# The last stage of a graph layer: routing and combining seven groups of nodes in three parts in place of two

## The chip, the cores and the metric

The kernel runs on one core of a Trainium2 chip. The metric is the time of one execution on the device in microseconds. Three executions of the kernel before took 3125.85, 3130.18 and 3136.21 us, a median of 3130.18 us.

## The reference

One layer of a graph transformer on 6250 nodes of 256 features, in float32. Cut to its frame and to the end of its feed-forward half, which is what the last stage computes:

```python
xn = _layernorm(x, axis=-1)
x = x + _L0_gnn_ref(xn, src, dst, ...) + _L0_mix_ref(xn[None], ...)[0]      # 100000 edges, linear attention
x = x + _L0_ffn_ref(_layernorm(x, axis=-1)[None], ...)[0]                   # 131072 edges + loops
...
# inside _L0_ffn_ref: h has 4 heads x 4 experts = 16 numbers per node
agg = segment_sum(msg, dst).reshape(M, 16) + b_gat                          # softmax-weighted over incoming edges
scores = _layernorm(agg, ln_gamma, ln_beta).reshape(M, HEADS, NUM_EXPERTS).mean(1)
topk_s, topk_i = lax.top_k(scores, 2)
w = softmax(topk_s)
out = 0
for ei in range(4):
    g = where(topk_i == ei, w, 0).sum(-1)
    hh = gelu(x @ W1[ei] + b1[ei], approximate=False)
    out = out + g[..., None] * (hh @ W2[ei] + b2[ei])
```

## The kernel before, in words

The nodes are 49 tiles of 128 (6250 padded to 6272). The long stages ahead, which gather rows for every edge and compute all four experts for every node, take the first 2981 us of the profile; they write two arrays to DRAM that the last stage reads: `state_ffn`, the running softmax state after every edge, and `y`, the four expert outputs of every node (4 x 256 numbers). `x1` holds the node features to which the result is added.

The last stage is the function `finish` (L2211). It splits the 49 tiles into 7 groups of G = 7 tiles. What each engine's program does there, in its own order:

- SP (L2260 to L2267) loads three small parameter rows, then `y` of group 0, then all of `x1` (`fin_x`, 6272 KB), then `y` of groups 1 and 2 (each 3584 KB). `fin_y` has three slots, so `y` of group b (b = 3 to 6) is loaded only once group b - 3 has been combined (semaphore `ready`).
- POOL (L2270 to L2275) issues 49 indirect gathers of the nodes' states, one per tile, in order of tiles. Each group has its own semaphore `got[q]`.
- DVE (L2325 to L2444) does for each group: `shift(q)` (L2336, waits for `got[q]`, three small operations), `merge(q)` (L2346, waits for ACT's exponentials, eight operations; it joins the gathered state with the node's own loop and divides). Within a part, `shift(q + 1)` comes before `merge(q)`. Once per part it does `route(part)` (L2364): a layer norm over the 16 numbers, the mean over heads, the ranks of the four experts, the two best and their weights. Each of its operations covers all tiles of the part at once, and behind nearly each comes a drain, since each reads what the last wrote. Then for each group of the part it does `combine(b)` (L2415): four tiles of the group by 16 scalar_tensor_tensor operations, and three tiles by adding what TensorE has mixed in PSUM.
- PE (L2278 to L2291) multiplies, for three tiles of each group, the four expert outputs by diagonal matrices of the gate weights. Each matmul of float32 operands is two instructions in the profile.
- ACT (L2293 to L2322) does the exponentials for the shifts (L2307), the square root and one exponential in each route (L2309, L2311; each ahead of them loads its table), the diagonal matrices (`spread_gates`, L2294, 12 activations for a group, for the first group of a part only after `routed`), and issues the store of each combined group (L2319).

`PARTS` (L2219) lists the groups of each part. All three programs that loop over parts (ACT, DVE and the helper `tiles`) take it from there. Before, part 0 has groups 0 to 2 and part 1 has groups 3 to 6. The order on DVE is thus: shift and merge of groups 0 to 2, route of 21 tiles, combine of groups 0 to 2, shift and merge of groups 3 to 6, route of 28 tiles, combine of groups 3 to 6. Nothing else sets the order; there is no planner.

Of the kernel before, what the change touches and what calls it, by code (L numbers as in the profile page):

```python
# [101 lines left out]
class Kernel:  # L102
# [2108 lines left out]
    def finish(self, own_h, own_m, out):  # L2211
# [4 lines left out]
        C, S, K = g.cols, g.state, g.per_head  # L2216
        G = FFN_BLOCK
        groups = NT // G
        PARTS = ((0, 3), (3, groups))  # L2219
        BY_PE = (G - 3, G - 2, G - 1)  # L2220
        with ExitStack() as here:
            x, yv = self.fin_x, self.fin_y
# [34 lines left out]
            def tiles(part):  # L2257
                return slice(PARTS[part][0] * G, PARTS[part][1] * G)

# [33 lines left out]
            def _(act):  # L2293
                def spread_gates(b):  # L2294
                    for n, u in enumerate(BY_PE):
# [5 lines left out]
                        ins.then_inc(spread, 1)  # L2301
                for part, (first_group, end) in enumerate(PARTS):
                    at = tiles(part)
# [21 lines left out]
            def _(dve):  # L2325
# [105 lines left out]
                dve.memset(eps[:, :], EPS)  # L2431
                for part, (first_group, end) in enumerate(PARTS):
                    for q in range(first_group, end):
# [96 lines left out]
```

How the kernel before makes its waits and increments, by code:

```python
            @block.vector  # L204
            def _(dve):
                dve.memset(self.edge_src["ffn"][:, :], 0)
                for g in (GNN, FFN):
                    dve.memset(self.start_rows[g.name][:, :, 0:1], 1.0)
                    dve.memset(self.start_rows[g.name][:, NT, 1:1 + H], 0.0)
                dve.wait_ge(counted, 1)
                dve.tensor_copy(lane[:, :], lane_i[:, :])
                dve.tensor_copy(tile_at[:, :], tile_i[:, :])
                dve.tensor_copy(node_at[:, :], node_i[:, :])
# [36 lines left out]
            def sp_samples(sp):  # L251
                table = self.sample_dram[g.name]
                sp.dma_start(here[:, :], table[:, :]).then_inc(samples_in, 16)
                sp.wait_ge(above_clear, 1)
                sp.dma_start(above[1:P, :], table[0:P - 1, :]).then_inc(samples_in, 16)
# [9 lines left out]
            def dve_rise(dve):  # L265
                dve.wait_ge(samples_in, 32)
                dve.tensor_tensor(rise[:, :], here[:, :], above[:, :], ALU.subtract)
                dve.memset(parts[:, 0, S:S + 1], 1.0)
                dve.memset(parts[:, 1, S:S + 1], 0.0)
# [12 lines left out]
            def pe_samples(pe, later, banks):  # L283
                pe.wait_ge(first_made, 1)
                pe.wait_ge(rise_ready, 1)
                for a, b, out in by_bank(banks):
                    for t in range(a, b):
# [4 lines left out]
            def dve_blocks(dve, banks, few):  # L293
                dve.wait_ge(samples_made, 1)
                for a, b, out in by_bank(banks):
```

## Time and profile before

| what | us |
|---|---|
| median of three executions | 3130.18 (3125.85 to 3136.21) |
| the profiled execution: its own time | 3130.82 |
| its span, first to last instruction | 3129.1 |
| last stage, from DVE's first operation in it to the end of the span | 2980.98 to 3129.1 |
| last operation of DVE ends | 3120.64 |

All positions are us from the span's start. A row of the chain or of the timeline has the start, the duration, the engine, the line and what the operation writes and reads; what stands in brackets is the idle time of the engine ahead of it and what ended that. An engine's name with a q (SPq, ACTq) is its issuing side: DMA issues stand there and aren't counted as busy.

### The profile page before, as it was taken

Reading aid. Unit: us, or ns where it says so; the run is one execution under the profiler, and the core shown is the slowest. Engines: PE = TensorE matmul, PEld = TensorE weight load, DVE = VectorE, ACT = ScalarE, POOL = GpSimd, SP = SyncE. Lnnn points to the kernel's source line nnn. Section 1 sums busy time; section 2 is a strip of 40 time slices with the busy share of each in tenths; the row PEclk is TensorE's granted clock in tenths of the full one; section 3 lists DMA queues with packets and bytes.
Section 4 is the critical chain, followed back from the end, with each engine's and each line's share of the span. In section 5 each row is a group of like instructions: output and inputs, shape, how many; then the busy total and the mean of one; then the engine's idle time right before and its main releaser. Section 6 shows DMA issues by size and latency. Waiting matters only on the chain. (4 is left out here: it accounts for less than half of the span.)

```text
span 3129.1 us, 19146 instructions
## 1 busy us (share of the span) xinstructions
PE 1313.0 (42%) x4490; PEld 883.1 (28%) x4490; DVE 1691.9 (54%) x2849; ACT 1207.3 (39%) x2380; POOL 2155.8 (69%) x2142
## 2 busy tenths in 40 slices
PE   2757611222222222221341566666666666661023
PEld 1523410111111111110330344444444444441012
DVE  7978899988888888884854111111111111111147
ACT  1522357766666676663430222222222222221012
POOL 0565657777777777776676777777777777777660
PEclk9878855555555555555555788888888888886557
DMA  4512646766666666665523122222222211122176
GB/s 130 189 54 74 194 135 227 235 209 209 217 212 216 220 211 210 211 218 189 165 61 100 30 42 42 42 42 42 42 42 42 42 37 37 36 42 47 17 255 247
DMA packets 223040, 392.05 MB, mean 125 GB/s; under 512 B 52803, under 2 KB 175346, under 8 KB 215504
## 3 DMA queue, kind: packets, MB, share of 16 engines
q1 hardware_dynamic: 132948, 258.07, 24.0%
q0 software_dynamic: 80880, 124.27, 16.9%
q10 hardware_dynamic: 9100, 8.50, 0.8%
q8 instruction: 36, 0.59, 0.1%
q14 instruction: 76, 0.62, 0.1%
HBM read 201.15 MB, written 189.55 MB: 125 GB/s over the span
## 5 line engine op out<-in xcount | busy, mean ns | idle before, releaser
L1217 POOL DMA_INDIRECT stage_got<-ffn_rows,setup_src_ffn x1024 | 985.0, 962 | 311.9 <-issue 311.9
L1217 POOL DMA_INDIRECT edges_got<-gnn_rows,edges_src_gnn x728 | 758.2, 1041 | 240.7 <-issue 221.5
L2099 PE MATMUL stage_ph<-ffn_xt_all,stage_w 128*128 128x448 f32 x896 | 408.1, 598 | 468.2 <-ACT stage_hid L2150 202.3
L1324 DVE TENSOR_TENSOR_SCAN stage_y<-stage_decays,stage_y 128x960 f32<-128x960 f32 (+2 forms) x256 | 521.1, 2090 | 5.1 <-issue 5.0
L1340 ACT ACTIVATE stage_rows<-stage_y 128x3640 f32<-128x3640 f32 (+1 forms) x88 | 399.9, 4544 | 0.0
L2099 PEld LDWEIGHTS stage_ph<-ffn_xt_all,stage_w 128*128 128x128 f32 x896 | 182.7, 208 | 615.2 <-ACT stage_start_parts L2150 203.8
L1233 DVE TENSOR_TENSOR stage_chunk_parts<-stage_got,edges_ffn_ed_edge 128x128 f32<-128x128 f32 x32 | 13.3, 416 | 592.3 <-DMA stage_got<-ffn_rows,setup_src_ffn 592.3
L1613 PE MATMUL stage_pm<-setup_ident,stage_mix_parts 128*128 128x128 f32 x98 | 33.4, 445 | 676.8 <-DVE stage_mix_parts L1686 604.2
L2176 DVE TENSOR_TENSOR search_found<-stage_po,stage_b 128x512 f32<-128x512 f32 x112 | 69.7, 625 | 420.9 <-PE stage_po L2110 416.1
L1282 ACT ACTIVATE stage_y<-stage_chunk_parts 128x56 f32<-128x56 f32 (+1 forms) x88 | 23.8, 271 | 670.4 <-DVE stage_chunk_parts L1254 669.9
L1300 DVE TENSOR_TENSOR stage_y<-edges_got,stage_y 128x896 f32<-128x896 f32 x168 | 262.9, 1671 | 0.3 <-ACT stage_y L1282 0.3
L1613 PEld LDWEIGHTS stage_pm<-setup_ident,stage_mix_parts 128*128 128x128 f32 x98 | 14.2, 204 | 706.4 <-DVE stage_mix_parts L1686 678.7
L1311 ACT ACTIVATE stage_y<-edges_got,stage_y 128x64 f32<-128x64 f32 x784 | 195.3, 388 | 0.0
L2110 PE MATMUL stage_po<-stage_w,stage_hid 128*128 128x256 f32 x784 | 189.9, 393 | 0.0
L2110 PE MATMUL stage_po<-stage_w,stage_start_parts 128*128 128x256 f32 x784 | 189.1, 393 | 0.0
L2110 PEld LDWEIGHTS stage_po<-stage_w,stage_hid 128*128 128x128 f32 x784 | 157.6, 201 | 51.4 <-issue 29.8
L2110 PEld LDWEIGHTS stage_po<-stage_w,stage_start_parts 128*128 128x128 f32 x784 | 157.4, 201 | 49.3 <-issue 27.5
L312 POOL DMA_INDIRECT search_found<-blocks_gnn,ject_search_gnn_at_block x50 | 53.9, 1077 | 113.5 <-DVE ject_search_gnn_at_block L306 98.6
L501 DVE TENSOR_TENSOR project_keys<-project_keys 128x512 f32<-128x512 f32 (+1 forms) x180 | 110.2, 612 | 25.3 <-ACT project_keys L471 14.0
L2150 ACT ACTIVATE stage_start_parts<-stage_ph,stage_b 128x896 f32<-128x896 f32 x56 | 54.9, 1005 | 165.9 <-PE stage_ph L2099 165.7
L2150 ACT ACTIVATE stage_hid<-stage_ph,stage_b 128x896 f32<-128x896 f32 x56 | 54.9, 1006 | 160.5 <-PE stage_ph L2099 160.4
L1617 PE MATMUL stage_pm<-stage_mix_parts 128*128 128x256 f32 x196 | 101.6, 674 | 23.2 <-ACT stage_mix_parts L1630 23.2
(465 smaller groups left out, 2588.7 us busy)
## 6 DMA issues: line engine op xcount, KB each, us to landing
state_gnn<-stage_rows SPq DMA_DIRECT2D x56, 1848.0 KB
y<-search_found SPq DMA_DIRECT2D x28, 896.0 KB, 4.2
tail_fin_y<-y SPq DMA_DIRECT2D x7, 3584.0 KB, 17.0
stage_got<-ffn_rows,setup_src_ffn POOLq DMA_INDIRECT x1024
edges_got<-gnn_rows,edges_src_gnn POOLq DMA_INDIRECT x784, 3.5
state_ffn<-stage_rows SPq DMA_DIRECT2D x32, 384.0 KB, 2.3
mix_rows<-stage_mix_parts SPq DMA_DIRECT2D x49, 131.0 KB, 2.1
x_again_mix<-mix_rows SPq DMA_DIRECT2D x7, 917.0 KB, 6.1
```

The costliest lines, as they stand in the source:

```text
L312: pool.indirect_dma_start(out=few[:, t, :], out_offset=None, in_=self.block_dram[g.name][:, :], in_offset=bass.IndirectOffsetOnAxis(ap=at_ ...
L501: dve.tensor_tensor(low, small, large, ALU.min)
L1217: pool.indirect_dma_start(out=got[:, u, t, :], out_offset=None, in_=self.row_dram[g.name][:, :], in_offset=bass.IndirectOffsetOnAxis(ap=sr ...
L1300: ins = dve.tensor_tensor(of_head(h, s)[:, :, :, 0:n].rearrange("p q k t -> p t q k"), mine.rearrange("p t (q k) -> p t q k", q=Q), w[:, h ...
L1311: ins = act.activation(of_head(h, s)[:, :, :, t], got[:, u, t, h * K:(h + 1) * K].rearrange("p (q k) -> p q k", q=Q), ACT.Copy, scale=y[:, ...
L1324: ins = dve.tensor_tensor_scan(some, r[s][:, 0:b - a, :].rearrange("p c t -> p (c t)"), some, 0.0, ALU.mult, ALU.add)
L1340: act.activation(rows[:, s, :, 0:C + H], y[:, s, :, 1:T + 1].rearrange("p c t -> p t c"), ACT.Copy).then_inc(rows_ready, 1)
L1617: mm = pe.matmul(pm[:, D:2 * D], qt[:, j * P:(j + 1) * P], cw[:, j, :], start=(j == 0), stop=(j == 1))
L2099: mm = pe.matmul(ph[:, f % 2 * 2 + half, 0:HALF], w1[:, e, k, f * P:(f + 1) * P], xt_all[:, k, at(b * (B * P) + half * HALF, HALF)], start ...
L2110: mm = pe.matmul(po[:, bank, side:side + D], hid[s][:, f, t * P:(t + 1) * P], w2[:, e, f, :], start=(f == 0), stop=(f == FT - 1))
L2150: act.activation(hid[s][:, f, :].rearrange("p (a n) -> p a n", a=2), ph[:, f % 2 * 2:f % 2 * 2 + 2, 0:HALF], ACT.Gelu, bias=b1[:, e, f:f + ...
L2176: dve.tensor_tensor(yrow[:, bank * 2:bank * 2 + n, :], po[:, bank, 0:n * D].rearrange("p (t d) -> p t d", d=D), b2[:, e, :].unsqueeze(1).t ...
```

## The change

One line. The seven groups are cut into three parts, of groups 0 and 1, groups 2 to 4, and groups 5 and 6:

```diff
@@ -2216,7 +2216,7 @@
         C, S, K = g.cols, g.state, g.per_head
         G = FFN_BLOCK
         groups = NT // G
-        PARTS = ((0, 3), (3, groups))
+        PARTS = ((0, 2), (2, 5), (5, groups))
         BY_PE = (G - 3, G - 2, G - 1)
```

The order on DVE becomes: shift and merge of groups 0 and 1, route of 14 tiles, combine of groups 0 and 1; shift and merge of groups 2 to 4, route of 21 tiles, combine of groups 2 to 4; shift and merge of groups 5 and 6, route of 14 tiles, combine of groups 5 and 6. The number of shifts, merges, combines, loads, gathers and stores is unchanged; `route` runs three times in place of twice, on DVE and on ACT.

## Rows read from the trace of the kernel before

**Rows 1.** The page, section 1: busy us of each engine over the span.

```profile
PE 1313.0 (42%) x4490; PEld 883.1 (28%) x4490; DVE 1691.9 (54%) x2849; ACT 1207.3 (39%) x2380; POOL 2155.8 (69%) x2142
```

**Rows 2.** Stretches of the last stage: length, busy us, PEclk, DMA share, GB/s.

```profile
core 0: us, PE busy (x) PEld busy (x) DVE busy (x) ACT busy (x) POOL busy (x), PEclk, DMA share, GB/s
3004.44:3007.61 3.17, 0.00 (x0) 0.00 (x0) 2.18 (x11) 0.25 (x1) 2.35 (x3) 0.50 1.10 338
3007.61:3014.04 6.43, 0.00 (x0) 0.00 (x0) 0.00 (x0) 0.00 (x0) 4.99 (x5) 0.50 1.10 331
3014.04:3018.96 4.92, 0.00 (x0) 0.00 (x0) 3.93 (x19) 1.53 (x2) 3.83 (x4) 0.50 1.04 384
3018.96:3034.05 15.09, 0.00 (x0) 0.00 (x0) 11.42 (x40) 1.95 (x4) 11.44 (x13) 0.50 1.00 378
3034.05:3044.19 10.14, 8.86 (x28) 7.36 (x29) 7.87 (x19) 6.98 (x24) 7.90 (x8) 0.65 0.10 12
3044.19:3052.24 8.05, 6.96 (x33) 5.84 (x32) 7.68 (x19) 3.62 (x12) 1.16 (x1) 1.00 0.88 299
...
3060.28:3071.43 11.15, 0.00 (x0) 0.00 (x0) 8.57 (x45) 2.28 (x5) 0.00 (x0) 0.50 1.04 414
3071.43:3087.68 16.25, 0.00 (x0) 0.00 (x0) 12.64 (x40) 1.88 (x4) 0.00 (x0) 0.50 0.54 213
3087.68:3096.64 8.96, 7.63 (x28) 6.52 (x29) 7.78 (x19) 7.07 (x24) 0.00 (x0) 0.74 0.01 2
...
3112.73:3120.64 7.91, 3.75 (x18) 2.95 (x16) 7.68 (x19) 0.00 (x0) 0.00 (x0) 0.93 0.35 117
3120.64:3129.10 8.46, 0.00 (x0) 0.00 (x0) 0.00 (x0) 0.00 (x0) 0.00 (x0) 0.50 0.33 106
```

**Rows 3.** Timeline of DVE, the wait for the states of group 2.

```profile
3014.04 0.19 DVE L2339 TENSOR_TENSOR finish_node_parts<-finish_st,stage_by_node 128x28 f32<-128x28 f32 x1 [6.51 <-DMA finish_st<-state_ffn,setup_end_at_ffn]
```

**Rows 4.** Timeline of DVE: starts of the merges of groups 2, 3 and 4.

```profile
3016.84 0.30 DVE L2351 TENSOR_TENSOR finish_node_parts<-finish_st,finish_d 128x112 f32<-128x112 f32 x1
...
3061.66 0.28 DVE L2351 TENSOR_TENSOR finish_node_parts<-finish_st,finish_d 128x112 f32<-128x112 f32 x1 [0.17 <-issue]
...
3064.30 0.28 DVE L2351 TENSOR_TENSOR finish_node_parts<-finish_st,finish_d 128x112 f32<-128x112 f32 x1 [0.17 <-issue]
```

**Rows 5.** Lines by form on DVE, routes of 21 and 28 tiles: busy us, mean ns.

```profile
L2327 DVE TENSOR_TENSOR finish_route_parts<-finish_route_parts 128x336 f32<-128x336 f32 x6 | 3.1, 512 | 0.4
...
L2327 DVE TENSOR_TENSOR finish_route_parts<-finish_route_parts 128x448 f32<-128x448 f32 x6 | 3.8, 626 | 0.4
```

**Rows 6.** SP's loads of `y`: groups 0 and 1, then all seven; issue ns, landing.

```profile
L2201 SPq DMA_DIRECT2D tail_fin_y<-y x1: 433/433/433, 2982.2 to 2982.2; - x1
DMA to landing us min/median/max: 13.6/13.6/13.6
...
L2201 SPq DMA_DIRECT2D tail_fin_y<-y x1: 25799/25799/25799, 2983.3 to 2983.3; - x1
DMA to landing us min/median/max: 41.9/41.9/41.9
...
DMA to landing us min/median/max: 13.6/17.0/41.9
```

**Rows 7.** DMA packets by size in 3012 to 3014 and in 3014 to 3016.

```profile
DMA packets 679, 0.69 MB, mean 345 GB/s; under 512 B 24, under 2 KB 671, under 8 KB 679
...
DMA packets 315, 0.77 MB, mean 385 GB/s; under 512 B 41, under 2 KB 153, under 8 KB 315
```

**Rows 8.** Stretches at the start of combine(0) and combine(3), columns as in Rows 2.

```profile
3035.00:3041.00 6.00, 5.67 (x13) 4.54 (x14) 5.78 (x15) 6.00 (x21) 4.60 (x5) 0.50 0.10 11
3041.00:3044.00 3.00, 3.00 (x15) 2.65 (x14) 1.09 (x3) 0.03 (x1) 2.39 (x3) 0.98 0.10 10
3089.00:3092.00 3.00, 2.99 (x7) 2.46 (x8) 2.85 (x8) 3.00 (x11) 0.00 (x0) 0.50 0.02 5
3092.00:3096.00 4.00, 4.00 (x19) 3.47 (x19) 3.19 (x9) 2.75 (x10) 0.00 (x0) 0.96 0.00 0
```

**Rows 9.** Timeline of ACT: its issue of the store of group 2.

```profile
3060.22 0.46 ACTq L2319 DMA_DIRECT2D out_dram<-tail_fin_x  x1
```

## The prediction

> **What bounds the kernel now.** I read the busy times first: POOL leads with 69% of the span [rows 1], but that is the edge gathers of the earlier stages, which the change doesn't touch. So I went to the last stage and followed the chain of waits back from the end, then cut that stage into stretches at the starts of DVE's steps [rows 2]. From 3014.04 on the chain is DVE almost without a break: merges to 3018.96, route of 21 tiles 15.09 us, combine(0) 10.14, combine(1) 8.05, combine(2) the same, shifts and merges of four groups 11.15, route of 28 tiles 16.25, combine(3) 8.96, three more combines, the last ending at 3120.64. DVE is busy 7.68 of the 8.05 us of a combine and 11 to 13 us of a route; the rest is drains. What follows is 8.46 us of last stores [rows 2]. No stretch there is limited by DMA: the share is 0.10 in combine(0) and 0.01 in combine(3). The one real hole after DVE's first merge is 6.43 us, from 3007.61 to 3014.04, where DVE does nothing [rows 2]; the timeline says that it waits for the gathered states of group 2 [rows 3]. POOL issues the gathers at a steady pace there (5 in those 6.43 us), so the hole is the gathers' pace and not a queue.
>
> **The change part by part.** In the new order DVE doesn't wait for group 2 before its first route; it has shift and merge of groups 0 and 1, a route and two combines to do first. All shifts, merges and combines remain, so the sum is over four terms.
>
> *Term 1, the hole goes: -6.43 us.* After merge(0) ends at 3007.61 comes merge(1) at once. Its exponential follows shift(1) (the first operations of the stretch from 3004.44), and merge(0) lies between, so it is ready. What is late next? Merge(1) takes 2.12 us (merge(2) starts at 3016.84, the route follows at 3018.96) [rows 2, 4], so the route starts at 3009.73. By term 2 it takes 13.6 us, so combine(0) starts at 3023.3. It needs `x1` and `y` of group 0. `y` of group 0 lands 13.6 us after 2982.2, at 2995.8 [rows 6]. `x1` moves in 1 KB rows and `y` in 4 KB rows, and small packets give way to large ones in 3014 to 3016 (671 of 679 under 2 KB before, 153 of 315 then) [rows 7]; so `x1` is in by about 3014, 9 us early. combine(1) starts at 3033.4, and `y` of group 1 lands at 2983.3 + 41.9 = 3025.2 [rows 6], 8 us early. Group 2's states are in at 3014.04, and shift(2) now comes at 3041.5. No wait takes the hole's place, so I take all of it. The bounds are 0 (a transfer ends the hole anyway) and 6.43.
>
> *Term 2, a third route: +10.3 us.* A route has 40 DVE operations whatever the size [rows 2]. The two sizes of the trace give the price per tile. Operations of 336 and 448 elements take 512 and 626 ns [rows 5]: 114 ns for 112 elements, 1.02 ns each, which leaves 170 ns fixed. By the code a route handles 214 elements per partition and tile (8 operations of 16 per tile, 14 of 4, 4 of 3, 4 of 2, 10 of 1), so 0.22 us per tile, 1.53 us per group. The measured difference of the whole stretches is 16.25 - 15.09 = 1.16 us for a group [rows 2]; it mixes in small differences between the places, and I keep it as the other bound. With 1.53: 14 tiles at the first place 15.09 - 1.5 = 13.6; 21 tiles at the later place 16.25 - 1.5 = 14.7; 14 tiles there 13.2; sum 41.6 against 31.34 before, +10.3. With 1.16: 13.9 + 15.1 + 13.9 = 42.9, +11.6. If a route cost were wholly by tiles (no fixed part), it would be 10.1 + 12.2 + 8.1 = 30.4, -1.0; two rows speak against that, since 7 tiles more, a third more work, cost 8% more time. I take +10.3, nearest to the row of the most used form. ACT's share of a route (two activations, two table loads) was inside these stretches and comes along; the loads lie beside DVE's work in both.
>
> The Trainium skill gives such operations a fixed term too: "VectorE: DVE Perf Modes", section "The TRN2 errata — SBUF-src ops pay a fixed extra latency per instruction", has a table with 58 cycles plus one per element at 0.96 GHz, and says below it that local measurements come nearer to about 150 cycles. By the table's 58 cycles, 40 operations would cost 2.4 us fixed, and the change would come out as a small gain; by 150 they cost 6.3 us, to which drains come. This trace agrees with the larger figure: the row's 170 ns are 163 cycles.
>
> *Term 3, one more start of a part: +0.9 us.* The first combine of a part has to wait for gates spread only after the route, and meets PE at the lower clock. combine(3) takes 8.96 us, an inner combine 8.05 [rows 2]. That makes +0.91 for one more start. combine(0) takes 10.14: there PE runs at 0.50 of full speed (1.2 GHz) until 3041, 6 us, where at combine(3) it rises to the full level (2.4 GHz) after 3 us [rows 8]. Both times PE had been idle for tens of us. combine(2) and combine(5) are the new later starts; PE idles there for some 20 us or more, as before combine(3). Should both get the longer slow stretch, it is 2 x 1.18 = +2.4 more. Lower bound 0 (start as good as an inner combine), upper 3.3.
>
> *Term 4, shifts and merges in three runs: +0.4 us.* Inside a run a shift and a merge take 2.64 us (3061.66 to 3064.30) [rows 4]; four groups took 11.15 [rows 2], so three take 8.51 and two 5.87 at the later places. At the first place 3.17 + 2.12 = 5.29. Sum 19.67, before 3.17 + 4.92 + 11.15 = 19.24 [rows 2]. The bounds are 0 and 0.6.
>
> *What costs nothing.* SP's loads of `y` 3 to 6 are issued as combines end, each earlier than before relative to its use: group 6's slot comes free after combine(3), which is now an inner combine of part 1 (about 3082), and the load takes some 17 us (the median [rows 6]) against a need at 3118. Without that cover PE would wait for it, as it already does for a few us beside DVE's work before. POOL's order is the same. ACT's stores are issued at the same points behind each combine. The tail of 8.46 us follows the same last group and is unchanged.
>
> *Sum:* -6.43 + 10.3 + 0.9 + 0.4 = +5.2 us. In the profiled execution's frame, DVE ends at 3125.8, the span is 3134.3, and the execution 3130.82 + 5.2 = 3136.0. The profiled execution lies 0.6 us above the median of the three runs, so on the median the forecast is 3130.18 + 5.2 = **3135.4 us**. The terms' bounds, with the hole kept as gone, are -6.43 + 10.3 + 0 + 0 = +3.9 and -6.43 + 11.6 + 3.3 + 0.6 = +9.1.
>
> **The rivals.**
>
> *A, faster: the third route is nearly free.* If the cost of a route followed its tiles, DVE would lose only terms 3 and 4: -6.43 - 1.0 + 0.9 + 0.4 = -6.1, so 3124.1 us. The place is DVE's routes; it decides for faster as soon as the fixed part of a route is below 5.1 us (6.43 less 1.3). For it speaks that the new first route lies where DVE had nothing to do; against it the 40 operations and the two sizes in rows 2 and 5. The table of the Trainium skill, "VectorE: DVE Perf Modes", same section as above, would point to this side.
>
> *B, slower: ACT gets stuck at a store.* ACT issues the store of a part's last group ahead of the exponentials for the next part's shifts, and there is one more such boundary. An issue can block: SP's load of `y` 1 took 25.8 us to issue with two large loads ahead of it [rows 6]. If the store of group 4 (about 3090) blocked until `y` 6 has landed (3082 + 17), DVE would wait for its exponentials for 9 us more: +14, 3144 us. It decides (beyond 0.3%) from 4.2 us of blocking on. Against it: before, the store of group 2 was issued at 3060.22 in 0.46 us with two loads of `y` still in flight [rows 9].
>
> *C, clock:* both later starts get combine(0)'s long slow stretch: +5.2 + 2.4 = +7.6, 3137.8 us.
>
> *D, the change doesn't remove the wait:* `x1` or `y` 1 hold up the early combines by as much as the hole was. +5.2 + 6.4 = +11.6, 3141.8 us. Against it stand 9 and 8 us of slack.
>
> **How the numbers follow.** Chances: forecast 0.72, A 0.06, B 0.06, C 0.12, D 0.04. A measurement of this kernel tells about 0.3% (9.4 us) from no change; the three runs themselves spread over 10.4 us. The forecast and C lie inside that on the slower side, B and D beyond it, A inside it on the faster side. With some 3 to 4 us of scatter between two medians, the forecast passes +9.4 about one time in eight, C one in three: 0.09 + 0.04 + 0.05 + 0.02 = 0.20 for slower, 0.03 for faster (A and scatter), 0.77 for the same. The range of 8 in 10 takes the bounds +3.9 and +9.1 and the scatter: 3128.5 to 3142.
>
> **What would show it.** In the changed kernel's trace: DVE's wait for group 2's states is gone and the hole between merges is under 0.5 us; a route of 14 tiles takes 13.2 to 13.9 us at both places, one of 21 tiles 14.7 to 15.1; 120 route operations in place of 80; combine(0) starts near 3023 without a wait for a DMA; combine(2) and combine(5) take about 9.0 us (C: 10.1); ACT's store issues stay at 0.4 to 0.5 us (B: one is longer). I am wrong if the routes together take less than 36.5 us, or if DVE waits for a transfer in combine(0) or combine(1).

## The result

The changed kernel takes 3136.98 us (median of 12 executions, 3133.98 to 3144.9), the kernel before 3129.51 us on the same chip (12 executions, 3124.33 to 3136.21). The ratio of after to before is 1.0022, with a 95% interval of 1.0012 to 1.0031: slower by 6.9 us (3.8 to 9.7); the two medians by themselves lie 7.5 us apart. The forecast was +5.2 us and 3135.4 us, with a range of 3128.5 to 3142. One execution of 4042.05 us, of the last kernel of the experiments, is left out of its ratio; its cause is unknown.

The profiled execution of the changed kernel took 3135.3 us, with a span of 3133.6. The spans differ by 4.5 us, less than the last stage's loss, because the stages ahead, which are the same, don't end at the same time in every run: DVE's first operation of the last stage starts at 2979.11, before at 2980.98.

```profile
2979.11 0.06 DVE L2431 MEMSET finish_route_parts<- 128x1 f32 x1 [3.66 <-PEq L144]
```

So the last stage is best measured from a point of its own: from the start of shift(1) to the end of DVE's last operation. Before that is 3004.44 to 3120.64, 116.20 us; after, 3002.54 to 3124.96, 122.42 us: +6.22. The stretches of the changed kernel, cut at the starts of DVE's steps as in [rows 2] (length, busy us of each engine, PEclk, DMA share, GB/s):

```profile
core 0: us, PE busy (x) PEld busy (x) DVE busy (x) ACT busy (x) POOL busy (x), PEclk, DMA share, GB/s
3002.54:3007.80 5.26, 0.00 (x0) 0.00 (x0) 3.90 (x20) 1.53 (x2) 4.04 (x5) 0.50 1.10 332
3007.80:3021.21 13.41, 0.00 (x0) 0.00 (x0) 9.75 (x40) 1.94 (x4) 10.36 (x11) 0.50 1.06 369
3021.21:3031.25 10.04, 8.76 (x28) 7.32 (x29) 7.89 (x20) 6.98 (x24) 7.60 (x9) 0.66 1.03 389
3031.25:3039.29 8.04, 4.58 (x22) 3.69 (x20) 7.68 (x19) 0.00 (x0) 6.21 (x7) 0.94 0.86 317
3039.29:3047.57 8.28, 0.00 (x0) 0.00 (x0) 6.56 (x34) 2.03 (x4) 3.70 (x4) 0.50 1.05 413
3047.57:3062.52 14.95, 0.00 (x0) 0.00 (x0) 11.06 (x40) 1.87 (x4) 0.00 (x0) 0.50 0.60 240
3062.52:3072.40 9.88, 8.56 (x28) 7.17 (x29) 7.87 (x19) 7.07 (x24) 0.00 (x0) 0.67 0.01 2
...
3088.49:3094.40 5.91, 0.00 (x0) 0.00 (x0) 4.38 (x23) 1.78 (x3) 0.00 (x0) 0.50 1.04 415
3094.40:3107.44 13.04, 0.00 (x0) 0.00 (x0) 9.47 (x41) 1.86 (x4) 0.00 (x0) 0.50 0.38 141
3107.44:3117.05 9.61, 8.29 (x28) 6.95 (x29) 7.87 (x19) 7.06 (x24) 0.00 (x0) 0.69 0.00 0
3117.05:3124.96 7.91, 4.58 (x22) 3.69 (x20) 7.69 (x19) 0.00 (x0) 0.00 (x0) 1.00 0.34 116
3124.96:3133.60 8.64, 0.00 (x0) 0.00 (x0) 0.00 (x1) 0.00 (x0) 0.00 (x0) 0.62 0.33 105
```

Read them in pairs with [rows 2]. The stretch of 6.43 us in which DVE did nothing has no counterpart: merge(1) follows merge(0), and the first route starts at 3007.80. In its place stands a third route. Where each microsecond of the 6.22 comes from:

| term | forecast | measured | from the stretches |
|---|---|---|---|
| the hole ahead of group 2's states | -6.43 | -6.43 | gone |
| routes | +10.3 | +10.06 | 13.41 + 14.95 + 13.04 = 41.40, before 15.09 + 16.25 = 31.34 |
| first combines of the parts | +0.9 | +2.38 | 10.04 + 9.88 + 9.61, before 10.14 + 8.96 and one inner combine of 8.05 |
| shifts and merges | +0.4 | +0.21 | 5.26 + 8.28 + 5.91 = 19.45, before 19.24 |
| sum | +5.2 | +6.22 | |

The waits of DVE from 3003 to the end show that no transfer took the hole's place: none of them is for a DMA, and the largest are for PE in the combines and for ACT inside the routes (total us, times, longest).

```profile
DVE tail_fin_x L2427 <- PE finish_mixed L2288: 4.7, 5, 1.3
DVE finish_route_parts L2327 <- ACT finish_route_parts L2309: 1.1, 3, 0.4
DVE finish_route_parts L2327 <- ACT finish_route_parts L2311: 0.8, 3, 0.3
DVE finish_node_parts L2351 <- issue: 0.7, 4, 0.2
```

The first of these lines holds most of the term that was sized too small. Before, DVE waited 2.7 us for PE in three places; now it is 4.7 us in five.

### The profile page after: what moved, and what is told of

It is laid out like the page before. It is cut to its first block and busy times, and to the rows that moved or that the text cites. A ratio compares the mean times of both kernels' runs of the same rounds, so it can differ in the third digit from the quotient of the medians.

```text
span 3133.6 us, 19230 instructions
## 1 busy us (share of the span) xinstructions
PE 1317.5 (42%) x4490; PEld 885.6 (28%) x4490; DVE 1698.8 (54%) x2889; ACT 1210.2 (39%) x2384; POOL 2155.2 (69%) x2142
```

## The experiments

All times are ratios to the kernel before on the same chip, with a 95% interval; before had a median of 3132.33 us beside the kernel of four parts, the kernel before with idle matmuls and the last kernel of this section, and 3132.7 us beside the other four. "The stage" is again the time from the start of shift(1) to DVE's last end in the kernel's own profile (before: 116.20 us). It is the sharper measure here.

**Two parts of 2 and 5 groups: the hole goes, without a third route.**

```diff
-        PARTS = ((0, 3), (3, groups))
+        PARTS = ((0, 2), (2, groups))
```

> Two parts as before, but of 2 and 5 groups: the hole ahead of group 2's states should go without a third route. My theory (hole -6.4 us, third route +10.1, third start of a part +2.4, shifts and merges +0.2): only the hole's term acts, routes together stay at about 31.3 us (14 tiles 13.4, 35 tiles 17.8), the second start of a part may cost 1 us more than before (9.9 in place of 9.0). DVE's last operation would come about 5.5 us earlier than in the kernel before. A new wait may take back up to 2 us: y of group 6 is loaded only after combine(3), which is now followed by two combines instead of three. So -3.5 to -5.5 us, 3124 to 3126 where before is 3129.5. Rival D (the early route merely meets another wait, the hole's time is not won): 0 us, a wait of 6 us for a DMA in combine(0) or combine(1).

Measured: ratio 0.9982 (0.9971 to 0.9992), median 3126.79 us, 5.6 us faster. The stage takes 113.04 us, 3.2 less than before. Its stretches:

```profile
3013.08:3026.49 13.41, 0.00 (x0) 0.00 (x0) 9.76 (x41) 1.95 (x4) 10.36 (x11) 0.50 1.06 370
3026.49:3036.28 9.79, 8.51 (x28) 7.15 (x29) 7.89 (x20) 6.97 (x24) 7.48 (x8) 0.68 1.03 389
...
3058.67:3076.53 17.86, 0.00 (x0) 0.00 (x0) 14.23 (x40) 1.89 (x4) 0.00 (x0) 0.50 0.15 57
3076.53:3086.91 10.38, 9.06 (x28) 7.43 (x29) 7.87 (x19) 7.07 (x24) 0.00 (x0) 0.64 0.00 0
...
3110.92:3112.95 2.03, 0.00 (x0) 0.00 (x0) 0.01 (x1) 0.00 (x0) 0.00 (x0) 1.00 1.07 381
```

The two routes take 13.41 + 17.86 = 31.27 us, as the two before (31.34), though cut elsewhere. The hole's 6.43 us are won and 2.03 us of them are given back ahead of combine(6), where DVE waits for `y` of group 6, with the DMA share at 1.07; that is the new wait that the expectation named. Another 0.8 us wait for the states of group 6 was not expected, and the two first combines take 1.1 us more than the two before (9.79 + 10.38 against 10.14 + 8.96). So the expected 3.5 to 5.5 us were a little too much for the stage, while the ratio, with 2.5 to 9.1 us in its interval, can't tell 3.2 from 5.6. Rival D, a wait in combine(0) or combine(1), is refuted here and in the changed kernel.

**Three parts of 3, 2 and 2 groups: the third route, with the hole kept.**

```diff
-        PARTS = ((0, 3), (3, groups))
+        PARTS = ((0, 3), (3, 5), (5, groups))
```

> Three parts of 3, 2 and 2 groups: the third route is there, the hole ahead of group 2's states is kept. My theory: +10 us for the third route, +1 to +2 for one more start of a part, +0.2 for shifts and merges, no gain: +11 to +12.5 us on before, 3141 to 3142, about 5.5 to 6.4 us above the changed kernel. Rival (a route costs by its tiles, and the changed kernel is slower because it meets new waits): equal to before or 1 us above it.

Measured: ratio 1.0039 (1.0027 to 1.0051), +12.2 us, median 3144.88 us. The stage takes 127.43 us, 11.2 more than before and 5.0 more than the changed kernel. The hole is there again, and each route costs what it cost at its size elsewhere:

```profile
3009.53:3015.97 6.44, 0.00 (x0) 0.00 (x0) 0.00 (x1) 0.00 (x0) 4.98 (x5) 0.50 1.11 333
...
3020.88:3035.99 15.11, 0.00 (x0) 0.00 (x0) 11.43 (x41) 1.96 (x4) 11.45 (x13) 0.50 1.00 377
3035.99:3044.90 8.91, 7.63 (x28) 6.52 (x29) 7.77 (x20) 6.98 (x24) 6.92 (x7) 0.74 0.12 12
3066.53:3079.90 13.37, 0.00 (x0) 0.00 (x0) 9.45 (x40) 1.86 (x4) 0.00 (x0) 0.50 1.04 413
3079.90:3089.06 9.16, 7.83 (x28) 6.66 (x29) 7.78 (x20) 7.07 (x24) 0.00 (x0) 0.73 0.09 32
3102.99:3116.02 13.03, 0.00 (x0) 0.00 (x0) 9.46 (x40) 1.86 (x4) 0.00 (x0) 0.50 0.15 55
3116.02:3125.88 9.86, 8.54 (x28) 7.17 (x29) 7.87 (x19) 7.07 (x24) 0.00 (x0) 0.67 0.00 0
```

With the two-part kernel this splits the change cleanly: a third route costs, the hole pays part of it back. The rival is refuted.

**Four parts of 2, 2, 1 and 2 groups: one more split.**

```diff
-        PARTS = ((0, 3), (3, groups))
+        PARTS = ((0, 2), (2, 4), (4, 5), (5, groups))
```

> Four parts of 2, 2, 1 and 2 groups: one more split of the changed kernel's middle part, the hole gone as in it. Theory: a part costs its fixed price wherever it is cut: +10.1 us of route (14 + 7 tiles take 13.1 + 11.7 = 24.8 where 21 took 14.95, +9.9), +1.8 for one more start at the lower clock, +0.2 for shifts and merges: +12 us on the changed kernel, so 1.0022 + 0.0038 = 1.0060 of before. Rival (the routes' cost falls with their size and small routes are cheap): +3 us or less on the changed kernel, 1.003.

Measured: ratio 1.0048 (1.0035 to 1.0062), median 3147.97 us. The expected 1.0060 lies inside the interval near its end, the rival's 1.003 below it. The trace is sharper: the stage takes 134.65 us (3000.81 to 3135.46), 12.2 us more than the changed kernel, against 12 expected: 10.6 from the four routes (52.00 for 41.40) and 1.6 from the four starts of a part. A route of a single group of 7 tiles still costs 11.79 us, of which 7.88 are busy:

```profile
3077.40:3089.19 11.79, 0.00 (x0) 0.00 (x0) 7.88 (x40) 1.85 (x4) 0.00 (x0) 0.50 1.04 414
```

The kernel with parts of 1 and 6 groups, which comes next, adds a second route of 7 tiles and one of 42:

```profile
2996.52:3007.93 11.41, 0.00 (x0) 0.00 (x0) 7.97 (x40) 1.79 (x3) 8.76 (x9) 0.50 1.10 334
3050.16:3069.98 19.82, 0.00 (x0) 0.00 (x0) 15.82 (x40) 1.91 (x4) 0.00 (x0) 0.50 0.00 0
```

So a route of 7, 14, 21, 28, 35 and 42 tiles takes 11.4 to 11.8, 13.0 to 13.4, 15.0 to 15.1, 16.3, 17.9 and 19.8 us: 10 us and 1.6 us per group of seven tiles. In each of them DVE is idle for 3.4 to 4.0 us between its operations, whatever the size; what grows is its busy time, from 7.9 to 15.8 us.

**Parts of 1 and 6 groups: a miss.**

```diff
-        PARTS = ((0, 3), (3, groups))
+        PARTS = ((0, 1), (1, groups))
```

> Two parts of 1 and 6 groups. The holes ahead of group 1's and group 2's states are both filled. By DVE's work alone: route of 7 tiles 11.9 us, of 42 tiles 19.3, and combine(0) can't start before x1 has landed (about 3014 of the trace before), so DVE would end 11 us earlier. But only slot 0 is free early: y of groups 4, 5 and 6 are loaded after combines 1, 2 and 3, each 3584 KB with an 896 KB store beside it, some 11.5 us against 8.05 us for a combine. My theory: the transfers become the bound of the last three combines and take back 5 to 6 us, so -5 us, 3124 to 3125, with waits of DVE for y ahead of combine(5) and combine(6). Rival (DVE alone sets the end): -11 us, 3118.

Measured: ratio 1.0014 (1.0003 to 1.0024), median 3135.89 us, 4.4 us slower, where 5 us faster was expected and the rival had 11 us faster. Neither theory had that. From shift(0), the first step whose start the two orders share, to DVE's last end it takes 131.81 us (2993.18 to 3124.99), before 125.30 (2995.34 to 3120.64): 6.5 more. DVE's waits from 2999 on:

```profile
DVE finish_node_parts L2339 <- DMA finish_st<-state_ffn,setup_end_at_ffn: 11.8, 3, 5.6
DVE tail_fin_x L2420 <- DMA tail_fin_x<-x: 5.5, 1, 5.5
DVE tail_fin_x L2420 <- DMA tail_fin_y<-y: 5.1, 2, 3.1
```

The last two lines are what was expected, 5.5 us for `x1` and 5.1 for `y`. The first was overlooked: 11.8 us of waits for the states of groups 4, 5 and 6. POOL issues one gather every 1.3 us (5 in 6.43 us [rows 2]), the last of the 49 at 3042.10 in this kernel, and group 6's states let DVE go on at 3045.27. From its shift(1) at 3021.50 on, at 2.64 us a group, DVE would have wanted them at about 3033. The hole isn't filled by starting earlier, it moves to the end of the same queue of gathers. The last route starts only after the last gather, whatever is done first.

**The clock of PE: idle matmuls through the routes.** PE waits for the variances of a route (`var_ready`), then multiplies the identity by ones into a PSUM bank that nothing reads, until about the time when the gates come. Nothing of the result changes.

```diff
+            warm = self.ps(here, "warm", [P, 512])
...
                 for b in range(groups):
                     s = b % Y_SLOTS
+                    for part, (first_group, _) in enumerate(PARTS):
+                        if b == first_group:
+                            pe.wait_ge(var_ready, part + 1)
+                            for _ in range(40):
+                                pe.matmul(warm[:, 0:P], self.ident[:, :], self.ones[:, :], start=True, stop=True)
                     pe.wait_ge(self.fin_y_in[s], 16 * (b // Y_SLOTS) + 16)
```

In the changed kernel:

> The changed kernel (2, 3, 2), but PE does 40 idle matmuls of 128 columns (ident by ones, into a PSUM bank of their own that nobody reads) from the moment DVE has the variances of each route, so that its clock is at the full level when the gates come. Theory: the start of a part costs more than an inner combine only because PE mixes at the lower clock: the three first combines fall from 10.0, 9.9 and 9.6 us to 8.1 to 8.4, together -5 us, 3132 where the changed kernel has 3137. Rival: the first combine is long because the gate matrices of ACT come only after the route (12 activations, 3.6 us), whatever the clock: the first combines stay at 9.6 to 10 us and the time at 3137.

Measured: ratio 1.0004 (0.9993 to 1.0014), median 3133.45 us, 5.6 us below the changed kernel's 1.0022. The stage takes 118.10 us, 4.3 less. The three first combines:

```profile
3020.51:3028.58 8.07, 7.41 (x38) 6.44 (x37) 7.71 (x19) 6.98 (x24) 6.24 (x7) 1.00 1.03 390
3059.96:3068.98 9.02, 7.70 (x28) 6.53 (x29) 7.77 (x19) 7.06 (x24) 0.00 (x0) 0.81 0.00 0
3103.99:3112.03 8.04, 6.79 (x32) 5.98 (x32) 7.68 (x20) 7.06 (x24) 0.00 (x0) 1.00 0.00 0
```

Two are down to the 8.05 us of an inner combine, with PE at the full level (2.4 GHz) throughout. The middle one isn't: its route has 21 tiles and outlasts the 40 matmuls, PE idled 2.1 us ahead of the gates, and the granted clock fell back to the lower level (1.2 GHz) just after, while PE was already mixing:

```profile
3059.00:3061.00 2.00, 0.18 (x2) 0.00 (x0) 1.73 (x6) 1.10 (x4) 0.00 (x0) 1.00 0.00 0
3061.00:3062.00 1.00, 0.72 (x3) 0.68 (x4) 0.93 (x3) 1.00 (x5) 0.00 (x0) 1.00 0.00 0
3062.00:3065.00 3.00, 3.00 (x9) 2.44 (x8) 2.93 (x8) 3.00 (x12) 0.00 (x0) 0.54 0.00 0
```

That failure is a control: the gates come as late after the route in all three parts, and only the one at the lower clock is long. The rival (ACT's gates) is refuted.

In the kernel before, with 48 and 52 idle matmuls in its two routes:

> The kernel before (3 and 4 groups) with PE kept busy through each route (48 and 52 idle matmuls). Theory: the first combines fall from 10.1 and 9.0 us to 8.1, -2.9 us, ratio 0.9991; y of group 6 lands 14.4 us after combine(3), so combine(6) then waits for nothing new or 0 to 1 us. Rival (the lower clock costs nothing once both parts have it): ratio 1.0000, first combines as before.

Measured: ratio 0.9989 (0.9978 to 0.9999), median 3128.65 us. The first combines take 8.05 and 8.04 us, the stage 113.26 us (3005.02 to 3118.28), 2.9 less than before, as expected. No wait for `y` appears.

**Both gains together: parts of 2 and 5 groups and 40 and 56 idle matmuls.**

> Parts of 2 and 5 groups, and PE kept busy through each route by idle matmuls (40 in the route of 14 tiles, 56 in that of 35), so that it mixes at the full clock when the gates come. Theory: both gains add. The first combines fall from 9.8 and 10.4 us to 8.1 each, -4.0 us on the two-part kernel of 2 and 5 (which measured 0.9982 of before); DVE's wait of 2.0 us for y of group 6 stays about as long, because its load is issued after combine(3), which moves with the rest. So -9.5 us on before, ratio 0.9970. Rival: the wait for y 6 grows by what the clock saves (the load is bound by the transfers, not by combine(3)): -5.6 us, ratio 0.9982, a wait of 5 to 6 us ahead of combine(6).

Measured: ratio 0.9976 (0.9965 to 0.9988), median 3125.18 us, 7.5 us faster than before and the lowest ratio of all kernels here, though its interval overlaps that of parts of 2 and 5 alone. The stage takes 110.12 us (3006.12 to 3116.24), 6.1 less than before but only 2.9 less than without the idle matmuls, where 4.0 was expected:

```profile
3024.81:3032.87 8.06, 6.78 (x32) 6.02 (x33) 7.70 (x19) 6.98 (x24) 6.23 (x7) 1.00 1.03 391
3074.86:3082.91 8.05, 7.51 (x38) 6.58 (x38) 7.69 (x19) 7.06 (x24) 0.00 (x0) 1.00 0.00 0
...
3052.07 0.19 DVE L2345 TENSOR_TENSOR finish_node_parts<-finish_st,stage_by_node 128x28 f32<-128x28 f32 x1 [2.29 <-DMA finish_st<-state_ffn,setup_end_at_ffn]
...
3108.30 6.91 DVE L2426 SCALAR_TENSOR_TENSOR tail_fin_x<-tail_fin_y,finish_route_parts,tail_fin_x 128x256 f32<-128x256 f32 x16 [1.37 <-DMA tail_fin_y<-y]
```

Both first combines are at 8.05 us, 4.1 us saved (from 9.79 and 10.38). But most of what is saved in combine(0) is lost again: DVE arrives earlier at the states of group 6 and waits 2.29 us for them (0.8 without the idle matmuls). The wait for `y` 6 stays short, 1.37 us, which refutes the rival. The total time doesn't separate the theory from the rival, whose 0.9982 lies in the interval; the waits in the trace do.

## Why the prediction was right, and where it was off

*The hole* was sized right, 6.43 us, and won in full; what was late next was nothing, as forecast. The early combines met their data: in the kernel with one group in the first part DVE's wait for `x1` ends at 3013.46, 33.1 us after the issue of that load at 2980.38. The estimate of about 3014 from packet sizes [rows 7] was 31.3 us after the issue at 2982.71 of the trace before, so 1.8 us too early; the changed kernel issues it at 2980.83 and needs it only at 3021.21, 40.4 us later. The kernels with and without the hole confirm it as a term: 3, 2, 2 groups take 5.0 us more in the stage than 2, 3, 2, where 6.4 less the shorter first combines (27.93 us in the one, 29.53 in the other) gives about 5.

*The third route* was forecast at +10.3 us and took +10.06. The step that carried it was to read two sizes of one operation [rows 5] and split them into 170 ns fixed and 1.02 ns per element. The new size tests it: 224 elements should take 170 + 228 = 398 ns, and take 393 (line, shape, count, busy us, mean ns).

```profile
L2327 DVE TENSOR_TENSOR finish_route_parts<-finish_route_parts 128x224 f32<-128x224 f32 x6 | 2.4, 393 | 0.4
```

Rival A needed a fixed part below 5.1 us; the routes of 7 to 42 tiles put it at 10: some 6.8 us of it are 40 times 170 ns, by estimate, and the rest the gaps between the operations. The 58 cycles in the table of the Trainium skill ("VectorE: DVE Perf Modes", section "The TRN2 errata — SBUF-src ops pay a fixed extra latency per instruction") don't describe this kernel; the page's own correction to about 150 cycles comes near the 163 of [rows 5].

*One more start of a part* was the term that was mis-sized: "I take +0.9", from combine(3) of the kernel before, where +2.38 came. The mechanism was named (PE mixes at the lower clock until it rises), and so was the bound of 3.3; the choice of the row was wrong. I took combine(3)'s short stretch at the lower clock for that of all later starts and combine(0)'s long one for a property of the first. The runs show that it is neither. Stretches at the start of the three parts in the changed kernel, to be read beside [rows 8]:

```profile
3022.00:3028.00 6.00, 5.50 (x13) 4.46 (x14) 5.78 (x15) 6.00 (x22) 4.78 (x5) 0.50 1.03 389
3063.00:3069.00 6.00, 5.16 (x12) 4.20 (x13) 5.78 (x16) 6.00 (x22) 0.00 (x0) 0.50 0.01 3
3108.00:3113.00 5.00, 4.24 (x10) 3.43 (x11) 4.78 (x12) 5.00 (x19) 0.00 (x0) 0.50 0.00 0
```

PE was at 0.50 for over 5 us of its work at the two former starts and for over 4 at the last. And combine(0) of the kernel with 3, 2, 2 groups, whose program is the same up to there as that of the kernel before, takes 8.91 us where that took 10.14 [rows 2]. The same code shows both. Over the eight starts whose rows stand here from the changed, the two-part and the 3, 2, 2 kernel the mean is 9.7 us, so 1.6 to 1.7 us a start, and that is the number to forecast with. The others without idle matmuls agree: 9.71, 10.12, 9.02 and 10.37 us with four parts, 10.07 at the second start with 1 and 6 groups. Rival C, given 0.12, was nearly what happened in size (+7.6 against +6.2 to 6.9). That the forecast came as near on the other side is in part luck: the routes and the shifts and merges came out 0.2 us each below their terms, the starts 1.5 us above theirs.

*Shifts and merges* (+0.21 for +0.4) and the unchanged tail (8.64 for 8.46 us) were right within what the trace scatters. Rival B didn't occur: ACT's issue of the store of group 4 is not followed by a late exponential; the shifts and merges of groups 5 and 6 take 5.91 us, with 5.87 forecast.

Open: why the lower clock lasts 3 us at one start and nearly 6 at another; and whether the total's 6.9 us differs from the stage's 6.2 + 0.2 by more than chance (the interval of 3.8 to 9.7 doesn't say so).

## What to carry to other kernels

A phase made of many short dependent operations has a price of which a large part doesn't depend on how much it handles (10 of 11.4 to 19.8 us here): read it at two sizes in the trace, and compare its fixed part with the hole that one more split would fill (6.4 us). Move the cut before adding one: two parts of 2 and 5 groups fill the same hole without a third route, for 3.2 us less in the stage; of the hole's 6.4 us the rest went to later waits and longer starts. And when a step is pulled ahead, look not only at what it needs first but at the last item of each queue that feeds it (here 49 gathers at 1.3 us each, and the last `y` block), since that item sets the next bound.

## What the runs showed that I had not expected

A start at PE's lower clock lasts unequally long in identical code: combine(0) took 10.14 and 8.91 us in the two kernels whose first part has three groups, and 10.04, 9.79 and 9.71 us in the three where it has two. Idle matmuls through the wait removed the excess wholly at six starts (8.04 to 8.07 us). At the seventh, where PE was idle for 2.1 us between the last of them and the first real one, the clock was still granted in full at first and fell within about a microsecond of the real work (9.02 us).
